# A cross-attention and quantised feed-forward kernel: four PSUM banks for the row maxima with a signal for each bank, the projection and the turned maxima moved inside the rings of banks, and the value product moved to the end of a key tile

## The reference, cut to what matters

```python
q = q * cos + rotate_half(q) * sin
k = k * cos + rotate_half(k) * sin
attn = jnp.einsum('bhqd,bhkd->bhqk', q, k) * scale
attn_w = jax.nn.softmax(attn, axis=-1)
out = jnp.einsum('bhqk,bhkd->bhqd', attn_w, v)
out = out.transpose(0, 2, 1, 3).reshape(B, S, D)
out = jnp.einsum('bsd,ed->bse', out, Wo) + bo
x = x + jnp.tanh(g_xattn[0]) * attention(layernorm(x), ctx, ctx, ...)
x = x + jnp.tanh(g_ffn[0]) * feed_forward(layernorm(x), ...)
```

## Time and profile before

| | |
|---|---|
| median of three runs | 639.18 us |
| time of the profiled execution | 641.87 us |
| its span on the core | 640.0 us |
| share of the span busy: PE, DVE, ACT, POOL | 89%, 86%, 69%, 41% |
| mean granted TensorE clock | 0.947 |

### The profile page before, as it was taken

One profiled execution on the slowest core, in us unless ns is written; L12 is line 12 of the kernel. 1 busy time (PEld: TensorE's weight loads), 2 busy tenths in 40 slices (PEclk: granted clock), 3 DMA queues, 4 the chain that ended last, 5 costly groups with the idle time before them and its releaser, 6 DMA issues. The chain is left out here.

```text
span 640.0 us, 18888 instructions
## 1 busy us (share of the span) xinstructions
PE 572.1 (89%) x6473; PEld 275.9 (43%) x6478; DVE 549.8 (86%) x935; ACT 441.5 (69%) x886; POOL 264.2 (41%) x372
## 2 busy tenths in 40 slices
PE   3999997999899989999999999999999983878485
PEld 1655554233344434444444444444444421433164
DVE  2799999899999869899899899899799757498878
ACT  2666766247677757787787687687687691688694
POOL 3898897601233434214214214214214202699400
PEclk9899999569999979999999999999999997799889
DMA  8559876522422224223223224224211000000025
GB/s 284 191 164 293 240 205 192 149 52 62 81 62 53 72 46 85 50 63 87 50 60 86 53 57 86 55 54 85 60 53 48 3 2 2 0 2 0 0 89 176
DMA packets 61256, 55.21 MB, mean 86 GB/s; under 512 B 11040, under 2 KB 58784, under 8 KB 61216
## 3 DMA queue, kind: packets, MB, share of 16 engines
q1 hardware_dynamic: 61216, 54.70, 33.0%
HBM read 37.62 MB, written 16.78 MB: 85 GB/s over the span
## 5 line engine op out<-in xcount | busy, mean ns | idle before, releaser
L864 DVE TENSOR_REDUCE negm<-mx_ps 128x1 f32<-128x512 f32 x512 | 319.3, 677 | 33.9 <-PE mx_ps L682 31.2
L805 ACT ACTIVATE prob<-st_ps 128x512 f32<-128x512 f32 x512 | 278.7, 597 | 98.3 <-PE st_ps L673 96.5
L682 PE MATMUL mx_ps<-k,q 96*32 96x512 bf16 x2048 | 221.4, 401 | 4.7 <-PEq L311 3.1
L673 PE MATMUL st_ps<-q,k 98*32 98x512 bf16 x2048 | 214.5, 386 | 4.8 <-ACT prob L805 3.5
L695 PE MATMUL pv_ps<-prob,v_u 128*32 128x512 f32 x1024 | 135.7, 598 | 8.6 <-DVE turned L873 5.8
L682 PEld LDWEIGHTS mx_ps<-k,q 96*32 96x32 bf16 x2048 | 64.0, 97 | 107.9 <-DVE negm L864 72.6
L673 PEld LDWEIGHTS st_ps<-q,k 98*32 98x32 bf16 x2048 | 68.8, 97 | 83.2 <-ACT prob L805 49.7
L1031 POOL TENSOR_TENSOR msplit<-negm,onesf 128x16 bf16<-128x16 f32 x32 | 7.1, 221 | 148.2 <-DVE negm L864 137.5
L1051 POOL TENSOR_TENSOR normal<-turned,recip 128x256 f32<-128x256 f32 x32 | 19.9, 621 | 99.5 <-DVE recip L879 99.5
L695 PEld LDWEIGHTS pv_ps<-prob,v_u 128*32 128x32 f32 x1024 | 32.5, 110 | 34.1 <-ACT prob L805 21.7
L298 POOL TENSOR_TENSOR parts<-work 128x512 bf16<-128x512 f32 x32 | 38.3, 1206 | 7.5 <-DVE work L286 6.0
(11 more groups left out here) (129 smaller groups left out, 729.0 us busy)
## 6 DMA issues: line engine op xcount, KB each, us to landing
qk_parts<-parts SPq DMA_DIRECT2D x96, 128.0 KB, 2.7
k<-qk_parts SPq DMA_DIRECT2D x192, 64.0 KB, 2.7
q<-qk_parts SPq DMA_DIRECT2D x192, 64.0 KB, 2.9
ctx<-in_ctxT SPq DMA_DIRECT2D x8, 512.0 KB, 4.4
X<-in_x SPq DMA_DIRECT2D x8, 512.0 KB, 7.9
out<-X SPq DMA_DIRECT2D x7, 512.0 KB, 2.9
q<-mrow SPq DMA_DIRECT2D x64, 4.0 KB, 2.5
wf<-in_w_down SPq DMA_DIRECT2D x1, 704.0 KB, 4.4
```

The costliest lines, as they stand in the source:

```text
L673: last = nc.tensor.matmul(st_ps[bank(i)][lo:lo + COLS, :], k6[g][:, h, kt * P + lo:kt * P + lo + COLS], q6[g][:, h, :], start=True, stop=True)
L682: last = nc.tensor.matmul(mx_ps[bank(i)][lo:lo + COLS, :], q6[g][0:ROWS, h, qt * P + lo:qt * P + lo + COLS], k6[g][0:ROWS, h, :], start=Tr ...
L805: nc.scalar.activation(prob[kt % 2][:, h, :], st_ps[bank(HPU * kt + h)][:], ACT.Exp, scale=SCALE).then_inc(exp_done, 1)
L864: nc.vector.tensor_reduce(negm[g % 2][:, h * TPB + qt:h * TPB + qt + 1], mx_ps[bank(TPB * h + qt)][:], op=ALU.max, axis=AX.X, negate=True) ...
```

## The change

1. `mx_ps` becomes two tiles of two banks each: four banks for the row maxima instead of three. Query scores are issued in pairs: after the scores of heads 0 and 2, two query scores each, one for each bank of a tile. Each bank is waited for by itself, and each signals by itself. `pair_bank` says which tile a pair uses.
2. `misc_ps` is gone. The turned maxima take a slot in the ring of the three `st_ps` banks, between the fourth and the fifth score tile of a unit (`TURN_SLOT`, `turn_bank`), and `wait_score_bank` holds the waits. The projection goes into the first bank of `mx_ps0` (hf = 0) or `mx_ps1` (hf = 1), once the pair that was there has been read. In the units g = 1 and 2 the two tiles swap their order from key tile 2 on.
3. `weigh` of the key tile before moves from ahead of the fourth head's scores to the end of the key tile. `take_max` on ACT moves from key tile 1 to the end of key tile 0. `residual` on DVE moves from behind the first two maxima of key tile 2 to ahead of them.

```diff
-        mx_ps = [ps(psB, f"mx_ps{i}", [P, S]) for i in range(2)]
-        misc_ps = ps(psB, "misc_ps", [P, 512])
+        mx_ps = [ps(psB, f"mx_ps{i}", [P, 2, S]) for i in range(2)]
         pv_ps = ps(psB, "pv_ps", [P, S])
-        mx_ps.append(ps(psB, "mx_ps2", [P, S]))
         st_ps = [ps(psB, f"st_ps{i}", [P, S]) for i in range(3)]
-        def bank(i):
-            return i % 3 if i < 15 else 1
+        TURN_SLOT = HPU
+        PROJ_PAIR = (0, 1)
+        def slot(i):
+            return i if i < TURN_SLOT else i + 1
+        def score_bank(i):
+            return st_ps[slot(i) % 3]
+        turn_bank = st_ps[TURN_SLOT % 3][0:2 * HPU * TPB, 0:P // 2].bitcast(BF16)
+        def wait_score_bank(eng, b, g, i):
+            n = 16 * (UPB * b + g)
+            if slot(i) == TURN_SLOT + 3 and not (is_last(b) and g == 3):
+                eng.wait_ge(mrow_ready, UPB * b + g + 2)
+            elif i < 3:
+                if not (is_first(b) and g == 0):
+                    eng.wait_ge(exp_done, n - 16 + (14, 15, 13)[i] + 1)
+            else:
+                back = next(j for j in range(16) if slot(j) == slot(i) - 3) if slot(i) != TURN_SLOT + 3 else 1
+                eng.wait_ge(exp_done, n + back + 1)
+        def pair_bank(g, kt, j):
+            return mx_ps[(2 * kt + j + (g == 2) + (g in (1, 2) and kt >= 2)) % 2]
...
-                def query_scores(b, g, h, qt):
-                    i = TPB * h + qt
-                    wait_bank_read(pe, mx_read, UPB * b + g, i)
-                    for lo in range(0, P, COLS):
-                        last = nc.tensor.matmul(mx_ps[bank(i)][lo:lo + COLS, :], ...)
-                    last.then_inc(mx_ready, 1)
+                def query_scores(b, g, h, j, pair, pairs_read):
+                    for qt in (2 * j, 2 * j + 1):
+                        if pairs_read is not None:
+                            wait_if(pe, mx_read, 2 * (pairs_read - 1) + qt % 2 + 1)
+                        for lo in range(0, P, COLS):
+                            last = nc.tensor.matmul(pair[lo:lo + COLS, qt % 2, :], ...)
+                        last.then_inc(mx_ready, 1)
+                def ahead_scores(b, g, kt, j):
+                    mb, mg = (b, g + 2) if g < 2 else (b + 1, g - 2)
+                    n = 8 * (UPB * mb + mg) + 2 * kt + j
+                    behind = g in (1, 2) and kt == 2
+                    if behind and j == 1 and not is_first(b):
+                        pe.wait_ge(x1_ready, 2 * (b - 1) + g)
+                    query_scores(mb, mg, kt, j, pair_bank(g, kt, j), (n - 1 if j else n) if behind else n - 1)
...
                 def project(b, hf):
-                    dst = misc_ps
+                    dst = project_bank(b, hf)
...
-                        max_taken(b, 1 + hf)
+                        pe.wait_ge(mx_read, 16 * (UPB * b + hf + 3) + 6)
...
                             for h in range(HPU):
-                                if h == HPU - 1:
-                                    if kt:
-                                        weigh(b, g, kt - 1)
-                                    elif not (is_first(b) and g == 0):
-                                        weigh(*((b, g - 1) if g else (b - 1, 3)), 3)
                                 scores(b, g, kt, h)
-                                if ahead:
-                                    query_scores(mb, mg, kt, h)
+                                if ahead and h in (0, 2):
+                                    ahead_scores(b, g, kt, h // 2)
+                            if kt:
+                                weigh(b, g, kt - 1)
+                            elif not (is_first(b) and g == 0):
+                                weigh(*((b, g - 1) if g else (b - 1, 3)), 3)
...
-                            if kt == 1 and not (is_last(b) and g == 3):
+                            exps(b, g, kt, (2, 3))
+                            if kt == 0 and not (is_last(b) and g == 3):
                                 take_max(b, g)
-                            exps(b, g, kt, (2, 3))
...
-                            if ahead:
-                                maxima(mb, mg, kt, (0, 1))
-                            if kt == 1 and not (is_first(b) and g == 0):
-                                invert_sums(b, g)
                             if kt == 2 and g in (1, 2) and not is_first(b):
                                 residual(b, g - 1)
                             if ahead:
-                                maxima(mb, mg, kt, (2, 3))
+                                maxima(mb, mg, kt, 0, pair_bank(g, kt, 0))
+                            if kt == 1 and not (is_first(b) and g == 0):
+                                invert_sums(b, g)
+                            if ahead:
+                                maxima(mb, mg, kt, 1, pair_bank(g, kt, 1))
```

More of the change, by code:

```diff
@@ L778, in _ @@
                     for h in range(HPU):
[L779 to L790 removed]
+                        for j in range(2):
+                            query_scores(0, g, h, j, mx_ps[j], 8 * g + 2 * h + j - 1)
+                        if g == 0 and h >= 2:
+                            c = h - 2
+                            if c == 0:
+                                pe.wait_ge(bv_ready, KC)
+                            last = nc.tensor.matmul(wobv_ps, bv_rep[:, c, :], wo_raw[:, c, :], start=(c == 0), stop=(c == KC - 1))
+                            if c == KC - 1:
+                                last.then_inc(wobv_ready, 1)
+                        if g and h == 0:
+                            pe.wait_ge(bo_ready, 1)
+                            max_transpose(0, -1)
                 over_batches(pe, body, B, True)
@@ L977, in _ @@
                 for h in range(HPU):
-                    maxima(0, 0, h, range(TPB))
+                    for j in range(2):
+                        maxima(0, 0, h, j, mx_ps[j])
                 dve.wait_ge(wobv_ready, 1)
-                nc.vector.tensor_tensor(bo_b[:], misc_ps[:, 0:D], bo_raw[:], ALU.add).then_inc(bo_ready, 1)
+                nc.vector.tensor_tensor(bo_b[:], wobv_ps, bo_raw[:], ALU.add).then_inc(bo_ready, 1)
                 for h in range(HPU):
-                    maxima(0, 1, h, range(TPB))
+                    for j in range(2):
+                        maxima(0, 1, h, j, mx_ps[j])
                 dve.wait_ge(bo_ready, 1)
```

72 lines of the change are left out of this document (27 added, 45 removed).

## The result

The changed kernel takes 618.98 us (median of 4 runs, 617.88 to 620.75), the kernel before 639.43 us in the runs made beside it (4 runs, 638.22 to 639.73). The ratio is 0.9692, with a 95% interval of 0.9665 to 0.9718. The forecast was 628.9 us with a range of 622 to 637: the direction is right, and the gain is twice what was forecast, 20.4 us for 10.3.

What follows compares the result with a forecast made beforehand. DVE (44.8 us a batch) and PE (45.4) were both near the bound, losing time waiting on each other. Batches 2 to 6 -9.0, batch 1 -1.0, batch 7 -0.8, ahead -0.5, end +1.0: -10.3, giving 628.9 us, range 622 to 637.

Steps and rivals of the forecast that it cites:

- the long unit and the next: Batch 1, unit g = 3 (16.3 us) and its successor: ACT waits for POOL's weights conversion, so nothing is won.
- the value product's move: End of each key tile: PE still stands 0.1 to 0.25 us in g = 1 and 3, but it costs nothing.
- the two short waits: DVE's waits of 0.36 and 0.44 us per batch for query-score banks; four banks leave 0.1 us of these 0.80.
- The batch's work stays 44.8 us on DVE: Loop batch: no reduction is added or removed, so DVE's own work stays 48.4 - 3.6 = 44.8 us.
- The projection's gap: DVE's two waits behind the projections in a batch shrink from 2.76 to about 1.65 us (0.7 and 0.9).
- The other waits: DVE's 0.80 us per batch where PE was held with three banks; 0.1 us left, bounds 0 and 0.8.
- The turned maxima in the score ring: Seventh score tile waits for ACT's copy, with about 0.2 us spare; POOL's split has 0.5 us left; cost nothing.
- the rival that PE would stop there for 0.4 us in each unit: Late ACT copy or POOL split stops PE at the seventh score or turning: 0.4 us in 31 units, 641 us; chance 0.07.
- Batch 0, ahead of the first unit: The fourth bank covers a 0.63 us wait ahead of the first unit, -0.5 us; nothing won within batch 0.
- The last two units: No query scores; four scores come first, 0.3 us more in four or five key tiles: +1.0 us, bounds 0 and +2.5.
- More is won: Rival: the projection's wait vanishes too, batch near PE's 45.4 us, -3.0 us in six batches, 619 to 624 us; chance 0.09.
- Only the short waits go: Rival: projection gaps stay 1.3 us each, end costs 2 us; 0.5 us a batch, 635 to 638.5 us; chance 0.16.

Runs made afterwards that it cites:

- the two kernels with an edit on before: Kernel before with only the value product moved to the key tile's end, 643.22 us; kernel before with POOL's two means of X ahead of its weights conversion, 633.89 us.
- the edit to the means: POOL's two means of X put ahead of its long weights conversion in units g = 3: 614.99 us on the changed kernel, 633.89 us on the kernel before.

## Why the prediction was wrong

**By stretch.** The table has -20.2 us where -10.3 were forecast. Of the 10 us between, 4.5 lie in the batches of the loop, the first three units of batch 1 and the two of batch 7; 3.3 lie ahead of and in batch 0; 1.7 lie in the long unit and the next, which go with the clock; and 0.5 in the third block, where nothing was changed.

**The step that failed in the loop is the value product's move, costed at nothing, together with the fourth bank, credited with the two short waits.** I took DVE's queue as the thing that sets the batch and asked only whether the moved value product would hold DVE up. What it does is on PE's side. With it in the middle of the key tile, scores in turn and everything else as changed, PE stands 2.6 us a batch, 1.8 for exponentials and 0.9 for DVE's turning, and a fourth bank doesn't help: 48.01 and 48.00 us. With it at the end these stands go, and now the reads of banks bind: PE stands 2.0 us for them, and the batch is 47.39 us with three. Only then is the fourth bank worth something, 1.6 us. Either alone brings 0.0 and 0.6 us, both bring 2.2. I had split the gain by the waits that DVE's view lists, and these two parts have no separate shares. The stand for the turning was seen, but too small: it was read as 0.2 to 0.4 us in a unit and 0.4 in a batch, and by the starts it is 0.36 to 0.42 us in each of the four units, 1.6 in a batch. Why exponentials are late in the one order and not in the other, though ACT has 10 us of slack in a batch, no run shows.

**"The batch's work stays 44.8 us on DVE" was off by 0.9 us.** I had taken 48.4 less the listed waits of 3.6 us. In the changed kernel the same sum is 45.90 - 1.99 = 43.9 us, and DVE's busy time is 43.8 us. The view doesn't list waits below about 0.15 us, and they hide in the start-to-start time of reductions. Ten reductions in a row before, and fourteen after, in order of time:

```profile
290.65 6.35 DVE L864 TENSOR_REDUCE negm<-mx_ps 128x1 f32<-128x512 f32 x10
296.92 0.70 DVE L886 STREAM_TRANSPOSE attnT<-normal 128x512 f32<-128x512 f32 x1
```

```profile
267.58 8.45 DVE L887 TENSOR_REDUCE negm<-mx_ps 128x1 f32<-128x512 f32 x14
275.95 0.70 DVE L895 STREAM_TRANSPOSE turned<-pv_ps 128x512 f32<-128x512 f32 x1
```

Before it is 6.27 us to the next instruction, 0.627 each; after, 275.95 - 267.58 = 8.37, 0.598 each. The mean hides how it comes about: start by start most reductions of the kernel before are 0.598 us apart too, and two of these ten stand 0.12 and 0.21 longer. Over the batch seven such distances, 0.08 to 0.21 us each, make 0.9 us. By this sum the loop's miss is accounted for: forecast 46.6 us, and 0.9 less own work, 0.2 more at the projections, gives 45.9. So the waits of DVE were forecast nearly right and its work was not, and the credit for each part of the change was wrong.

**The projection's gap: right in mechanism, small in size.** The gaps were put at 0.7 and 0.9 us, ahead of the residual, and are 0.87 and 1.12. PE shows the chain as walked: scores, value product, a short stand, then the projection.

```profile
287.74 1.08 PE L719 MATMUL pv_ps<-prob,v_u 128*32 128x512 f32 x8
288.78 1.93 PE L766 MATMUL mx_ps<-woT,attnT 128*32 128x256 f32 x32
290.53 0.40 PE L687 MATMUL st_ps<-q,k 98*32 98x512 bf16 x4
```

From 287.74 the value product's 0.86 us ends at 288.60, and the projection starts 0.18 later, 0.05 us behind the end of the read that it waits for; the forecast had 0.14 for this release and 0.04 for the one back to DVE, where the residual starts 0.18 us behind the projection's end. The step named the residual only as cover for the next pair; that its new place is the condition for all of it was not seen.

**The other waits: right.** They were put at 0.1 us of what was 0.80; no wait of DVE for a query score is listed in the loop.

**The turned maxima in the score ring: nearly right.** No score waits at the seventh tile for ACT's copy. The four scores behind the turning start 0.00, 0.03, 0.03 and 0.12 us after it, the last just behind an exponential, so at most 0.2 us in a batch is lost where nothing was forecast, and the rival that PE would stop there for 0.4 us in each unit did not come about.

**Batch 0, ahead of the first unit: too small.** The maxima ahead of the first unit have the same short waits as the loop. The changed kernel runs 16 of them in one piece, where the earlier trace rows has a gap of 0.63 us ahead of the last four:

```profile
110.06 9.78 DVE L887 TENSOR_REDUCE negm<-mx_ps 128x1 f32<-128x512 f32 x16 [0.78 <-PE mx_ps L697]
```

With these and a wait of 0.44 us ahead of `bo_b` the stretch up to the second split lost 1.8 us, where 0.5 was forecast. It takes 22.3 to 22.5 us in the kernels with the rings of before, 21.5 to 21.7 with three banks' worth of waiting in the new rings, and 20.7 to 21.2 with four, so somewhat under half of the gain there is the fourth bank's. The first unit was costed at nothing because DVE is busy for 99% of a stretch of batch 0; it lost 1.6 us. It takes 12.1 and 12.2 us before, but 11.55 in the two kernels with an edit on before, though the edit to the means doesn't touch it; 10.7 to 11.2 with three banks in the rings; and 10.5 to 10.7 with four. The clock rises to 1.00 within this unit, between 0.8 and 4.2 us after its start, so which part is due to what isn't settled.

**Batch 1: the long unit and the next go with the clock.** Forecast at 0, the two together went from 28.18 to 26.51 us. In both profiles of the kernel before, the granted clock is 0.5 for 6.8 us of this stretch; in the three of the changed kernel it is 0.5 for 3.4, 0 and 3.4 us, and they take 26.51, 25.15 and 26.51 us. In all profiles without the edit to the means the two units take 25.2 to 25.6 us where the clock stays at 1.00, 26.4 to 27.1 with 3.4 us at 0.5, and 27.8 to 28.3 with 6.8, in the old order as in the new: three banks in the old order have 25.57 us, four have 28.19. So the measured 1.7 us can't be credited to the edits. With the means early they win 0.8 us there. Whether the edits make the clock fall later or less often, five profiles of two kernels don't show.

**The last two units: right.** +1.0 was forecast. From the split ahead of them to the last value product they take 23.34 us in both profiles of the kernel before and 24.40 or 24.41 in the three of the changed kernel, all at a clock of 1.00: +1.1. In the kernels of these experiments with the value product in the middle it is 23.34 us (scores in turn) and 23.94 (pairs), and 24.3 to 25.3 with it at the end, so its place is the cause, as forecast. Of the 1.1 us, 0.6 lies between the first score and the last value product; the rest is that the split now comes earlier against PE's scores. The third block behind them came out 0.5 us shorter in one profile and 1.2 longer in the next.

**The rivals.** "More is won" had the right region of times (619 to 624 us, against medians of 618.98, 620.57 and 620.33), and the batch did come near the floor of PE, 45.90 us to the 45.4 of the prediction. But its cause is wrong: the projection's gaps did not vanish, they are 1.99 us in a batch. "Only the short waits go" is false by those same gaps. The clock never fell in the loop of any kernel from the second unit of batch 2 on, 1.00 in the batch windows, also where PE stood twice a batch, for 1.33 and 1.36 us. By the rule on psum-queue cycling that the Trainium skill states (TensorE: Matmul & The Clock Gate, "A second HAM failure mode: psum-queue depth-cycling") it would have; the runs disagree for this kernel. The rule of the Trainium skill on repeated gaps and too little PSUM (Perfetto Trace Analysis, "Optimization Strategy") gave an estimate of 619 us, which is what came, but two of the four waits that it took away are still there, so the number is right by luck. The runs agree with the rule only in part: three banks in the changed order cost 3.25 us a batch (49.15 against 45.90), but a fourth bank in the old order brought 0.0.

## What to carry to other kernels

When two engines are both within some per cent of the length of a stretch, the listed waits of one of them are not its whole slack: hold its work against the shortest start-to-start time of its main instruction anywhere in the trace, and look at what the other engine stands for. An order of issue and the depth of a ring are to be costed together, because each can hide what the other would bring; the experiment that tells is all the combinations, not the whole less one part (which called the bank everything). And where a step moves into a ring's bank, look for the instruction that frees that bank on the other engine: here its place in the order decided whether the move paid.

## What the runs showed of the hardware

Reductions of 128 x 512 from PSUM start 0.598 us apart when nothing holds them, though each is listed at 0.672 us. PE starts a group 0.05 us behind the end of the reduction or exponential that it stood for, but a value product 0.15 us behind the end of a turning by DVE. The granted clock fell to 0.5 late in or behind the long stand of PE in batch 1 in most profiles, and not in all: with one of 2.82 us (kernel before) it was 0.5 for 6.8 us, behind one of 2.86 us (changed kernel) for 3.4 us, and behind one of 2.87 us (the same kernel again) it stayed at 1.00. The stands of 1.33 and 1.36 us in each batch of the kernel with the residual at its old place left it at 1.00. The first block's length moved by up to 3.6 us between profiles of kernels that agree in it, which is more than most of the effects here; without the cut by stretches it would have been put down to the edits.
